# The drain of a two-stage expert pipeline, reordered on four engines

## Chip, core and metric

One NeuronCore of a Trainium2 chip runs the whole kernel. The metric is the device time of one execution in microseconds; the median of several runs is given. The profile comes from one execution of its own.

## What is computed

For each of 128 samples of 64 rows and 256 columns, two layers run one after the other. Each sample has an index for each layer.

```
# layer 0: expert e = itok_B_0_7[b] of 8
h = gelu(x @ Wi[e] + bi[e])                 # 256 -> 1024
r = h @ Wo[e] + bo[e] + x                   # 1024 -> 256
x = layernorm(r, 1e-12) * gamma[e] + beta[e]
# layer 1: domain d = itok_B_0_15[b] of 16
a = gelu(x @ down_W.T + down_b)             # 256 -> 64
a = a @ expert_W[d].T + expert_b[d] + domain_emb[d]
x = layernorm(a @ up_W.T + up_b + x, 1e-5) * ln_gamma + ln_beta
```

## The kernel before

The samples are sorted by expert on the chip and laid into 68 tiles of two samples each (128 rows). A tile passes through a software pipeline: step `i` works on tiles `i` down to `i - 5` at once, on all engines, and each engine runs its own written order of operations; semaphores alone tie the engines together. Steps 0 to 67 start a tile each; steps 68 to 72 only finish tiles, and are called the drain here. Step numbers of the drain are Python integers, as are those from 64 on (from 66 on in SyncE's queue); earlier steps run in loops.

For a tile `t` the stages and the step in which they run:

- Step t, TensorE: first product into `p_h` (L929 to L931). ScalarE: gelu (L589) and rounding to 16 bits (`h_hi`, L597), in two halves. VectorE: the rest `h_lo` (L775), the first half in step t, the second in step t + 1.
- Step t + 1, TensorE: second product into the one bank `p_o` (L1028, then 24 matmuls L937 to L939). It may start when the residual sum of the tile before has been read out of `p_o`.
- Step t + 2, VectorE: residual sum r (L785), its statistics (L788, L797); GpSimd: variance to the power -1/2 (L488); VectorE: z = normalized r (L816), into the one buffer `z1`; TensorE: two transposes of z into `p_t` (L970), written between the two halves of the second product of tile t + 1; GpSimd: fetches gamma and beta of the expert into `gb_tile` (L496); ScalarE: `yT` from the transposes (L629).
- Step t + 3, TensorE: down projection (L948); ScalarE: gelu (L613) and 16 bit part (L616); VectorE: low part `a1s` (L805); GpSimd: `yg` = z times gamma of the expert (L483).
- Step t + 4, TensorE: up projection (L958, then four L962) into `p_u`; VectorE: second residual sum into `yg` (L794), statistics (L800, L808); GpSimd: power (L492); VectorE: normalized y (L825).
- Step t + 5, GpSimd: times the last gamma (L475), plus the last beta (L477); SyncE: two transfers to `out` (L379).

In one step the order on GpSimd is: L475 and L477, L483, L488, L492, L496, and where they exist the copies for tile i (L502, L461). On VectorE it is: L785, L788, L794, L797, L800, L805, L808, L775 (second half), L816, the low part of x, L825, and the first half L775. TensorE's step begins with loading registers and addresses for the weights; up and down projections lie inside the first product, and in the drain, where no first product exists, they stand at the beginning of the step. Before writing z for tile i - 2, VectorE waits for the transposes of the tile before and for GpSimd's multiply (L483) of the tile before (`need(dve, yg_done, i - 2)`).

Of the kernel before, what the change touches and what calls it, by code (L numbers as in the profile page):

```python
# [4 lines left out]
B, S, D = 128, 64, 256  # L5
# [3 lines left out]
KD, KI = D // P, I // P  # L9
# [29 lines left out]
def build(nc, t):  # L39
# [4 lines left out]
    with ctx:  # L44
# [6 lines left out]
        def sem(name):  # L51
            return ctx.enter_context(nc.semaphore(name))
# [190 lines left out]
        z2_done = sem("z2_done")  # L243
        zg_done = sem("zg_done")
        y_done = sem("y_done")

        block = ctx.enter_context(nc.Block())

# [27 lines left out]
        def run(eng, step, unroll=4, ahead=0):  # L276

            lead, mid = LEAD - ahead, CHUNKS - FIRST_CHUNKS - ahead
            for i in range(lead):
                j = i + ahead  # L280
                step(i, i % 2, i % 4, (j % NCH, (j + FIRST_CHUNKS) // NCH, j % SLOTS_W))
            tail = mid + (TILES - 2 - mid) // 4 * 4
            for begin, end, weights, times in ((lead, mid, True, unroll), (mid, tail, False, 4)):
                with eng.Fori(0, (end - begin) // times) as n:
                    i = eng.snap(n * times + begin)
                    for q in range(times):
                        step(i + q, q % 2, (begin + q) % 4,
                             (q, n + (FIRST_CHUNKS + LEAD) // NCH, (LEAD + q) % SLOTS_W) if weights else False)
            for i in range(tail, STEPS):
                step(i, i % 2, i % 4, False)  # L290

        def loads(i, parity, each):

# [13 lines left out]
        def _(sp):  # L307
# [59 lines left out]
            def step(i, parity, four, weights):  # L367
                if weights:
                    if weights[0] == 0:
                        expert[0] = first_chunk(weights[1])  # L370
                    load_later(i + AHEAD, expert[0], weights[0], weights[2])
                if exists(i + 2) or exists(i - 5):
                    b = indices(sp, 6 * i + IDX_SP, 6, SLOTS - 1)
                if exists(i + 2):
                    load_turned(inside(b[2:4]), i + 2, parity)
                if exists(i - 5):
                    sp.wait_ge(y_done, i - 4)
                    for n in range(2):
# [11 lines left out]
        def _(pool):  # L390
# [73 lines left out]

            def step(i, parity, four, weights):
                e_third, e_before, _, _, e_next = indices(pool, i + (IDX_EXP - 3), 5, E0 - 1)
                if exists(i - 5):

                    last = y[:, 1 - parity, :]
                    pool.wait_ge(z2_done, i - 4)  # L470

                    pool.wait_ge(hlo_half, 2 * min(i, TILES) - 1 if isinstance(i, int) else 2 * i - 1)
                    if isinstance(i, int) and i == 5:
                        pool.wait_ge(ln_in, 2 * 16)
                    pool.tensor_tensor(last, last, lng[:, :], ALU.mult).then_inc(zg_done, 1)  # L475
                    pool.wait_ge(zg_done, i - 4)
                    pool.tensor_tensor(last, last, lnb[:, :], ALU.add).then_inc(y_done, 1)  # L477
                if exists(i - 3):

                    if isinstance(i, int) and i == 3:  # L480
                        pool.wait_ge(g_in, 16)
                    pool.wait_ge(z1_done, i - 2)
                    pool.tensor_tensor(yg[:, 1 - parity, :], z1[:, :], g_t[:, bass.ds(e_third * D, D)], ALU.mult)\  # L483
                        .then_inc(yg_done, 1)
                if exists(i - 2):

                    pool.wait_ge(mv1_done, i - 1)
                    pool.tensor_tensor(rs[:, 0:1], mv[:, 0, 1:2], neg_half[:, 0:1], ALU.pow).then_inc(rs1_done, 1)  # L488
                if exists(i - 4):

                    pool.wait_ge(mv2_done, i - 3)
                    pool.tensor_tensor(rs[:, 1:2], mv[:, 1, 1:2], neg_half[:, 0:1], ALU.pow).then_inc(rs2_done, 1)  # L492
                if exists(i - 2):

                    need(pool, yT_done, i - 2)
                    pool.tensor_copy(gb_tile[:, :], gb_c[:, bass.ds(e_before * 2 * KD, 2 * KD)]).then_inc(gb_done, 1)  # L496
                if exists(i):

                    if isinstance(i, int) and i == 0:
                        pool.wait_ge(sel_ready, 1)  # L500
                    need(pool, up_done, i - 3)
                    pool.tensor_copy(sel_tile[:, four, :].rearrange("p (n s) -> p n s", n=2),  # L502
                                     sel[:, bass.ds(2 * i, 2)].unsqueeze(2).to_broadcast([P, 2, S]))\
                        .then_inc(sel_done, 1)
                if exists(i + 1):
                    gather_bi(e_next, i + 1, 1 - parity)
                if isinstance(i, int) and i == 1:
                    pool.wait_ge(u_ready, 1)
# [129 lines left out]
        def _(dve):  # L638
# [139 lines left out]
            def step(i, parity, four, weights):  # L778
                if isinstance(i, int) and i == 0:
                    dve.wait_ge(bo_ready, 1)  # L780
                if exists(i - 2):

                    dve.wait_ge(s2_done, i - 1)
                    dve.wait_ge(xnat_in[parity], loads(i - 2, parity, 2))
                    v.scalar_tensor_tensor(r1[:, :], p_o[:, 0:D], 1.0 / (HS * WS), x_nat[:, parity, :],  # L785
                                           ALU.mult, ALU.add).then_inc(r1_done, 1)
                    dve.wait_ge(r1_done, i - 1)
                    v.bn_stats(st1[:, 0:6], r1[:, :]).then_inc(st1_done, 1)  # L788
                    dve.wait_ge(st1_done, i - 1)
                if exists(i - 4):  # L790

                    dve.wait_ge(up_done, i - 3)
                    dve.wait_ge(yg_done, i - 3)
                    v.scalar_tensor_tensor(yg[:, parity, :], p_u[:, 0:D], 1.0 / (AS * CS), yg[:, parity, :],  # L794
                                           ALU.mult, ALU.add).then_inc(r2_done, 1)
                if exists(i - 2):
                    v.bn_aggr(mv[:, 0, :], st1[:, :]).then_inc(mv1_done, 1)  # L797
                if exists(i - 4):
                    dve.wait_ge(r2_done, i - 3)
                    v.bn_stats(st2[:, 0:6], yg[:, parity, :]).then_inc(st2_done, 1)  # L800
                    dve.wait_ge(st2_done, i - 3)
                if exists(i - 3):

                    dve.wait_ge(a1_hi, i - 2)
                    v.scalar_tensor_tensor(own(S), a1[S:P, :].rearrange("p (n s) -> p n s", n=2), AS, own(S),  # L805
                                           ALU.mult, ALU.subtract).then_inc(a1_lo, 1)
                if exists(i - 4):
                    v.bn_aggr(mv[:, 1, :], st2[:, :]).then_inc(mv2_done, 1)  # L808
                if exists(i - 1):
                    split_h(i - 1, 1 - parity, 1)  # L810
                if exists(i - 2):

                    dve.wait_ge(rs1_done, i - 1)
                    need(dve, tr_done, i - 2)
                    need(dve, yg_done, i - 2)
                    v.tensor_scalar(z1[:, :], r1[:, :], mv[:, 0, 0:1], rs[:, 0:1], ALU.subtract, ALU.mult)\  # L816
                        .then_inc(z1_done, 1)
                if exists(i + 1):
                    low_x(i + 1, 1 - parity)
                if exists(i - 4):  # L820

                    dve.wait_ge(rs2_done, i - 3)
                    if not isinstance(i, int) or i >= 6:
                        dve.wait_ge(y_out[parity], loads(i - 6, parity, 2))
                    v.tensor_scalar(y[:, parity, :], yg[:, parity, :], mv[:, 1, 0:1], rs[:, 1:2],  # L825
                                    ALU.subtract, ALU.mult).then_inc(z2_done, 1)
                if weights:

                    dve.wait_ge(w_hi, i + 1)
# [9 lines left out]
        def _(pe):  # L839
# [101 lines left out]
            def step(i, parity, four, weights):  # L941
# [85 lines left out]
                        pe.wait_ge(bo_ready, 1)  # L1027
                    mm(p_o[:, 0:D], sel_tile[:, (four + 3) % 4, :], bo_parts[:, :], start=True, stop=False)  # L1028
                for j in range(KI):
                    if j == TR_AT and exists(i - 2):  # L1030
                        transpose()
                    if exists(i - 1):
                        if j == KI // 2:
# [1 line left out]
                        ins = second_product(1 - parity, there, j)  # L1035
                        if j == KI - 1:
                            ins.then_inc(s2_done, 1)

            pe.wait_ge(idx_ready, TILE_READY)
            run(pe, step)  # L1040
# [47 lines left out]
```

## Time and profile before

| | us |
|---|---|
| median of 3 runs (498.99 to 499.26) | 499.21 |
| the profiled execution's own time | 498.85 |
| its span, first to last instruction | 497.1 |
| TensorE busy with matmuls | 473.9 (95%) |
| VectorE busy | 355.6 (72%) |
| GpSimd busy | 358.6 (72%) |
| mean granted clock of TensorE | 0.983 |

The span is the stretch between the first and the last instruction of the profiled execution; its own time holds 1.75 us around it. The profile names each operation by its line in the kernel, with start, duration, and in brackets how long the engine had been idle before it and what released it. PE is TensorE's matmuls, PEld its weight loads, DVE VectorE, ACT ScalarE, POOL GpSimd, SPq SyncE's queue.

### The profile page before, as it was taken

Reading aid. Unit: us, or ns where it says so; the run is one execution under the profiler, and the core shown is the slowest. Engines: PE = TensorE matmul, PEld = TensorE weight load, DVE = VectorE, ACT = ScalarE, POOL = GpSimd, SP = SyncE. Lnnn points to the kernel's source line nnn. Section 1 sums busy time; section 2 is a strip of 40 time slices with the busy share of each in tenths; the row PEclk is TensorE's granted clock in tenths of the full one; section 3 lists DMA queues with packets and bytes.
Section 4 is the critical chain, followed back from the end, with each engine's and each line's share of the span. In section 5 each row is a group of like instructions: output and inputs, shape, how many; then the busy total and the mean of one; then the engine's idle time right before and its main releaser. Section 6 shows DMA issues by size and latency. Waiting matters only on the chain.

```text
span 497.1 us, 19258 instructions
## 1 busy us (share of the span) xinstructions
PE 473.9 (95%) x5778; PEld 438.7 (88%) x5779; DVE 355.6 (72%) x936; ACT 373.8 (75%) x1099; POOL 358.6 (72%) x587
## 2 busy tenths in 40 slices
PE   4699999999999999999999999999999999999972
PEld 2399999999999999999999999999999999999961
DVE  6678777777777777777777777777777767666662
ACT  2588887777787778788777778877878877677651
POOL 6044787788778877788778877887778876667765
PEclk9799999999999999999999999999999999999996
DMA  4734343333343333333333333333343222222111
GB/s 117 269 83 117 93 91 105 100 95 99 102 106 105 86 99 100 98 96 103 103 88 95 99 100 99 102 86 102 97 100 79 63 55 66 64 58 55 39 44 32
DMA packets 70257, 45.84 MB, mean 92 GB/s; under 512 B 43969, under 2 KB 61778, under 8 KB 70098
## 3 DMA queue, kind: packets, MB, share of 16 engines
q1 hardware_dynamic: 69200, 45.25, 34.6%
q8 instruction: 15, 0.25, 0.2%
q10 hardware_dynamic: 1026, 0.21, 0.2%
q14 instruction: 16, 0.13, 0.1%
HBM read 36.51 MB, written 8.91 MB: 91 GB/s over the span
## 4 chain that ended last, share of the span: by engine, by line
PE 93%; DVE 3%; POOL 1%; issue 1%; DMA 0%; ACT 0%; POOLq 0%; DVEq 0%
PE p_h L929 13%; PE p_h L931 12%; PE p_h L930 12%; PE p_o L939 12%; PE p_o L938 12%; PE p_o L937 12%; PE p_d L948 7%; PE p_u L962 6%; PE p_t L970 3%; PE p_u L958 2%; PE p_o L1028 1%; PE p_h L872 1%; DVE W L737 1%; POOL y L475 0%; PE p_t L872 0%
## 5 line engine op out<-in xcount | busy, mean ns | idle before, releaser
L929 PE MATMUL p_h<-x_hi,W 128*128 128x128 f16 x1088 | 193.8, 220 | 0.0
L930 PE MATMUL p_h<-x_lo,W 128*128 128x128 f16 x1088 | 193.6, 220 | 0.0
L931 PE MATMUL p_h<-x_hi,W 128*128 128x128 f16 x1088 | 193.6, 220 | 0.0
L589 ACT ACTIVATE h<-p_h,bi_tile 128x128 f32<-128x128 f32 x544 | 152.6, 362 | 0.6 <-PE p_h L931 0.6
L938 PE MATMUL p_o<-W,h_hi 128*128 x544 | 148.3, 273 | 0.0
L939 PE MATMUL p_o<-W,h_lo 128*128 x544 | 148.3, 273 | 0.0
L937 PE MATMUL p_o<-W,h_hi 128*128 x544 | 148.3, 273 | 0.0
L492 POOL TENSOR_TENSOR rs<-mv,neg_half 128x1 f32<-128x1 f32 x68 | 59.7, 878 | 74.2 <-DVE mv L808 74.2
L929 PEld LDWEIGHTS p_h<-x_hi,W 128*128 x1088 | 107.0, 98 | 5.2 <-issue 3.8
L930 PEld LDWEIGHTS p_h<-x_lo,W 128*128 x1088 | 106.9, 98 | 2.1
L931 PEld LDWEIGHTS p_h<-x_hi,W 128*128 x1088 | 106.9, 98 | 0.0
L613 ACT ACTIVATE a<-p_d,downb 128x128 f32<-128x128 f32 x68 | 25.0, 367 | 90.0 <-PE p_d L948 90.0
L775 DVE SCALAR_TENSOR_TENSOR h_lo<-h,h_hi 128x512 f16<-128x512 f32 x136 | 91.1, 670 | 1.4 <-ACT h_hi L597 1.4
L597 ACT ACTIVATE h_hi<-h 128x512 f16<-128x512 f32 x136 | 86.1, 633 | 2.2
L502 POOL COPY sel_tile<-sel 128x128 f16 (+1 forms) x68 | 81.0, 1191 | 2.0 <-issue 2.0
L805 DVE SCALAR_TENSOR_TENSOR a1s<-a,a1s 64x128 f16<-64x128 f32 x68 | 19.7, 289 | 66.5 <-ACT a1s L616 66.4
L475 POOL TENSOR_TENSOR y<-y,lng 128x256 f32<-128x256 f32 x68 | 49.3, 726 | 20.5 <-DVE h_lo L775 18.7
L785 DVE SCALAR_TENSOR_TENSOR r<-p_o,x_nat 128x256 f32<-128x256 f32 x68 | 28.8, 424 | 44.2 <-PE p_o L939 44.1
L939 PEld LDWEIGHTS p_o<-W,h_lo 128*128 128x128 f16 x544 | 53.2, 98 | 6.2
L938 PEld LDWEIGHTS p_o<-W,h_hi 128*128 128x128 f16 x544 | 53.2, 98 | 6.2
L629 ACT ACTIVATE yT<-p_t,gb_tile 128x128 f32<-128x128 f32 x136 | 55.3, 461 | 3.7 <-PE p_t L970 2.1
L937 PEld LDWEIGHTS p_o<-W,h_hi 128*128 128x128 f16 x544 | 53.2, 98 | 4.7
(155 smaller groups left out, 814.3 us busy)
## 6 DMA issues: line engine op xcount, KB each, us to landing
stage<-in_w SPq DMA_DIRECT2D x56, 256.0 KB, 2.7
x_nat<-in_x SPq DMA_DIRECT2D x136, 64.0 KB, 2.1
out<-y SPq DMA_DIRECT2D x136, 64.0 KB, 2.0
x_T<-in_xT SPq DMA_DIRECT2D x134, 64.0 KB, 2.2
W<-in_w SPq DMA_DIRECT2D x8, 256.0 KB, 4.6
g_t<-in_gamma SPq DMA_DIRECT2D x1, 1024.0 KB, 7.8
W<-in_expert_W SPq DMA_DIRECT2D x2, 128.0 KB, 3.0
upT<-in_up_W SPq DMA_DIRECT2D x2, 64.0 KB, 2.7
```

What stands on the lines that cost most here:

```text
L492: pool.tensor_tensor(rs[:, 1:2], mv[:, 1, 1:2], neg_half[:, 0:1], ALU.pow).then_inc(rs2_done, 1)
L502: pool.tensor_copy(sel_tile[:, four, :].rearrange("p (n s) -> p n s", n=2), sel[:, bass.ds(2 * i, 2)].unsqueeze(2).to_broadcast([P, 2, S]))\
L589: ins = nc.scalar.activation(h[:, c, :], p_h[parity][:, c, :], ACT.Gelu, bias=bi_tile[:, parity, c:c + 1], scale=1.0 / (XS * WS))
L597: nc.scalar.activation(h_hi[:, parity, cols_h, :], h[:, cols_h, :], ACT.Copy, scale=HS)\
L629: ins = nc.scalar.activation(yT[:, k, :], p_t[:, k * P:k * P + P], ACT.Identity, bias=gb_tile[:, KD + k:KD + k + 1], scale=gb_tile[:, k:k ...
L775: v.scalar_tensor_tensor(h_lo[:, parity, cols_h, :], h[:, cols_h, :], HS, h_hi[:, parity, cols_h, :], ALU.mult, ALU.subtract).then_inc(hlo ...
L929: mm(p_h[parity][:, c, :], hi, x_hi[:, parity, k, :], start=(k == 0), stop=False)
L930: mm(p_h[parity][:, c, :], hi, x_lo[:, parity, k, :], start=False, stop=False)
L931: ins = mm(p_h[parity][:, c, :], lo, x_hi[:, parity, k, :], start=False, stop=(k == KD - 1))
L937: mm(p_o[:, 0:D], h_hi[:, parity, j, :], hi, start=False, stop=False)
L938: mm(p_o[:, 0:D], h_hi[:, parity, j, :], lo, start=False, stop=False)
L939: return mm(p_o[:, 0:D], h_lo[:, parity, j, :], hi, start=False, stop=(j == KI - 1))
```

## The change

All of it concerns the drain (steps 68 and later) and the outputs of the last four tiles (64 to 67). TensorE: the second product of tile 67 runs without the transposes in its middle; the transposes stand behind it. GpSimd in the drain: first the copy to `gb_tile`, then both powers, then the multiply by the expert's gamma, then the output's gamma and beta, and these last two not at all for the last four tiles. VectorE in the drain: a new order, beginning with the second half of `h_lo`, and for the last four tiles the output in two fused operations, (yg - mean) * ln_gamma and then times the power plus ln_beta. SyncE waits for a semaphore of its own for these four.

```
 GpSimd, step(i):
+                if drain(i):                    # i an int, i >= 68
+                    gather_gb()
+                    powers()
+                    scale_z()
+                    scale_out()                 # only if the tile i - 5 is none of the last four
+                else:
+                    scale_out()
+                    scale_z()
+                    powers()
+                    gather_gb()
...
 VectorE, step(i):
+                def late_gamma():
+                    dve.wait_ge(mv2_done, i - 3)
+                    dve.wait_ge(y_out[parity], loads(i - 6, parity, 2))
+                    v.scalar_tensor_tensor(y[:, parity, :], yg[:, parity, :], mv[:, 1, 0:1], lng[:, :],
+                                           ALU.subtract, ALU.mult).then_inc(yl_done, 1)
+                def late_out():
+                    dve.wait_ge(rs2_done, i - 3)
+                    dve.wait_ge(yl_done, i - 3 - (TILES - 4))
+                    v.scalar_tensor_tensor(y[:, parity, :], y[:, parity, :], rs[:, 1:2], lnb[:, :],
+                                           ALU.mult, ALU.add).then_inc(y_late, 1)
+                if drain(i):
+                    if exists(i - 1):
+                        split_h(i - 1, 1 - parity, 1)
+                    if exists(i - 2):
+                        residual_1()
+                        aggr_1()
+                    if exists(i - 4):
+                        residual_2()
+                        stats_2()
+                        aggr_2()
+                    if exists(i - 2):
+                        normal_1()
+                    if exists(i - 4):
+                        late_gamma()
+                    if exists(i - 3):
+                        low_a()
+                    if exists(i - 4):
+                        late_out()
+                    return
...
 TensorE, step(i), in and behind the second product:
-                    if j == TR_AT and exists(i - 2):
+                    if j == TR_AT and exists(i - 2) and not drain(i):
                         transpose()
...
+                if drain(i) and exists(i - 2):
+                    transpose()
...
 SyncE, step(i), in front of the output of tile i - 5:
-                    sp.wait_ge(y_done, i - 4)
+                    if late(i - 5):
+                        sp.wait_ge(y_late, i - TILES)
+                    else:
+                        sp.wait_ge(y_done, i - 4)
```

The functions `residual_1`, `aggr_1`, `residual_2`, `stats_2`, `normal_1` and `low_a` hold the operations that stood there before (L785 and L788, L797, L794, L800, L816, L805), `aggr_2` L808. Outside of the drain their order is the old one.

## Rows read from the trace of the kernel before

**Rows 1.** Page: the chain that ended last, shares of the span by engine.
```profile
PE 93%; DVE 3%; POOL 1%; issue 1%; DMA 0%; ACT 0%; POOLq 0%; DVEq 0%
```

**Rows 2.** Chain that ended last: start us, us, what.
```profile
491.27 0.56 POOL rs L492
...
493.11 0.76 POOLq L44
```

**Rows 3.** Timeline of VectorE, 476 us on: start us, us, operation, count.
```profile
476.92 0.42 DVE L785 SCALAR_TENSOR_TENSOR r<-p_o,x_nat 128x256 f32<-128x256 f32 x1 [1.21 <-PE p_o L939]
...
479.19 0.65 DVE L775 SCALAR_TENSOR_TENSOR h_lo<-h,h_hi 128x512 f16<-128x512 f32 x1
479.75 0.41 DVE L816 TENSOR_SCALAR z<-r,mv,rs 128x256 f32<-128x256 f32 x1
...
482.00 0.42 DVE L785 SCALAR_TENSOR_TENSOR r<-p_o,x_nat 128x256 f32<-128x256 f32 x1 [1.31 <-PE p_o L939]
...
484.27 0.37 DVE L816 TENSOR_SCALAR z<-r,mv,rs 128x256 f32<-128x256 f32 x1
...
488.12 0.29 DVE L805 SCALAR_TENSOR_TENSOR a1s<-a,a1s 64x128 f16<-64x128 f32 x1 [0.37 <-ACT a1s L616]
...
489.63 0.42 DVE L794 SCALAR_TENSOR_TENSOR yg<-p_u,yg 128x256 f32<-128x256 f32 x1
...
490.54 0.20 DVE L808 BATCH_NORM_AGGREGATE mv<-st 128x2 f32<-128x9 f32 x1
```

**Rows 4.** Timeline of TensorE (PE) and its weight loads (PEld), 477 us on.
```profile
477.60 0.10 PEld L1028 LDWEIGHTS p_o<-bo_parts,sel_tile 128*128 128x128 f16 x1
...
480.22 0.44 PE L970 MATMUL p_t<-ident,z 128*128 128x128 f32 x2 [0.93 <-DVE z L816]
...
481.69 0.27 PE L939 MATMUL p_o<-W,h_lo 128*128 x1
...
484.70 0.44 PE L970 MATMUL p_t<-ident,z 128*128 128x128 f32 x2 [1.75 <-DVE z L816]
486.09 0.10 PEld L958 LDWEIGHTS p_u<-parts,sel_tile 128*128 128x128 f16 x1 [1.19 <-issue]
...
486.23 0.60 PE L962 MATMUL p_u<-ctab,a1s 128*128 x4
...
488.47 1.03 PE L962 MATMUL p_u<-ctab,a1s 128*128 x4 [0.48 <-DVE a1s L805]
```

**Rows 5.** Timeline of GpSimd (POOL), 477 us on.
```profile
477.34 0.73 POOL L483 TENSOR_TENSOR yg<-z,g_t 128x256 f32<-128x256 f32 x1
...
479.35 0.89 POOL L492 TENSOR_TENSOR rs<-mv,neg_half 128x1 f32<-128x1 f32 x1 [0.36 <-DVE mv L808]
...
493.15 0.72 POOL L477 TENSOR_TENSOR y<-y,lnb 128x256 f32<-128x256 f32 x1
```

**Rows 6.** Timeline of ScalarE (ACT), 476 us on.
```profile
476.31 0.63 ACT L597 ACTIVATE h_hi<-h 128x512 f16<-128x512 f32 x1
```

**Rows 7.** Timeline of GpSimd and VectorE early in the run, 39.8 to 46 us.
```profile
39.87 0.68 DVE L737 SCALAR_TENSOR_TENSOR W<-stage,W 128x512 f16<-128x512 f32 x1
39.92 1.22 POOL L483 TENSOR_TENSOR yg<-z,g_t 128x256 f32<-128x256 f32 x1 [0.26 <-DVE z L816]
...
45.30 0.73 POOL L483 TENSOR_TENSOR yg<-z,g_t 128x256 f32<-128x256 f32 x1 [1.47 <-DVE z L816]
45.37 1.22 DVE L737 SCALAR_TENSOR_TENSOR W<-stage,W 128x512 f16<-128x512 f32 x1
```

**Rows 8.** Timeline of GpSimd and VectorE, 307 to 308 us.
```profile
307.14 0.50 DVE L825 TENSOR_SCALAR y<-yg,mv,rs 128x256 f32<-128x256 f32 x1
307.21 0.29 POOL L502 COPY sel_tile<-sel 128x128 f16 x1
```

**Rows 9.** Busy time by window: PE, PEld, DVE, ACT, POOL, granted clock, DMA.
```profile
487.00:487.25 0.25, 0.25 (x3) 0.08 (x1) 0.25 (x1) 0.00 (x0) 0.25 (x2) 1.00 0.00 0
487.25:487.50 0.25, 0.02 (x1) 0.00 (x0) 0.22 (x2) 0.19 (x1) 0.25 (x1) 0.69 0.00 0
```

More of the change, by code:

```diff
@@ L245, in build @@
         y_done = sem("y_done")
+        yl_done = sem("yl_done")
+        y_late = sem("y_late")
         block = ctx.enter_context(nc.Block())
@@ L290, in run, with drain, late @@
                 step(i, i % 2, i % 4, False)
+        def drain(i):
+            return isinstance(i, int) and i >= TILES
+        def late(j):
+            return isinstance(j, int) and TILES - 4 <= j < TILES
         def loads(i, parity, each):
@@ L466, in step @@
                 e_third, e_before, _, _, e_next = indices(pool, i + (IDX_EXP - 3), 5, E0 - 1)
[L467 to L496, printed above, removed]
+                def scale_out():
+                    if exists(i - 5) and not late(i - 5):
+                        last = y[:, 1 - parity, :]
+                        pool.wait_ge(z2_done, i - 4)
+                        pool.wait_ge(hlo_half, 2 * min(i, TILES) - 1 if isinstance(i, int) else 2 * i - 1)
+                        if isinstance(i, int) and i == 5:
+                            pool.wait_ge(ln_in, 2 * 16)
+                        pool.tensor_tensor(last, last, lng[:, :], ALU.mult).then_inc(zg_done, 1)
+                        pool.wait_ge(zg_done, i - 4)
+                        pool.tensor_tensor(last, last, lnb[:, :], ALU.add).then_inc(y_done, 1)
@@ new lines, in scale_z, with powers @@
+                def scale_z():
+                    if exists(i - 3):
+                        if isinstance(i, int) and i == 3:
+                            pool.wait_ge(g_in, 16)
+                        pool.wait_ge(z1_done, i - 2)
+                        pool.tensor_tensor(yg[:, 1 - parity, :], z1[:, :], g_t[:, bass.ds(e_third * D, D)], ALU.mult)\
+                            .then_inc(yg_done, 1)
+                def powers():
+                    if exists(i - 2):
+                        pool.wait_ge(mv1_done, i - 1)
+                        pool.tensor_tensor(rs[:, 0:1], mv[:, 0, 1:2], neg_half[:, 0:1], ALU.pow).then_inc(rs1_done, 1)
+                    if exists(i - 4):
+                        pool.wait_ge(mv2_done, i - 3)
+                        pool.tensor_tensor(rs[:, 1:2], mv[:, 1, 1:2], neg_half[:, 0:1], ALU.pow).then_inc(rs2_done, 1)
@@ new lines, in gather_gb @@
+                def gather_gb():
+                    if exists(i - 2):
+                        need(pool, yT_done, i - 2)
+                        pool.tensor_copy(gb_tile[:, :], gb_c[:, bass.ds(e_before * 2 * KD, 2 * KD)]).then_inc(gb_done, 1)
+                if drain(i):
[8 more added lines that the diff above has]
+                    gather_gb()
@@ L780, in step, with residual_1 @@
                     dve.wait_ge(bo_ready, 1)
-                if exists(i - 2):
+                def residual_1():
                     dve.wait_ge(s2_done, i - 1)
@@ L789, in step, with residual_2 @@
                     dve.wait_ge(st1_done, i - 1)
-                if exists(i - 4):
+                def residual_2():
                     dve.wait_ge(up_done, i - 3)
@@ L795, in step, with aggr_1, stats_2 @@
                                            ALU.mult, ALU.add).then_inc(r2_done, 1)
-                if exists(i - 2):
+                def aggr_1():
                     v.bn_aggr(mv[:, 0, :], st1[:, :]).then_inc(mv1_done, 1)
-                if exists(i - 4):
+                def stats_2():
                     dve.wait_ge(r2_done, i - 3)
@@ L801, in step, with low_a @@
                     dve.wait_ge(st2_done, i - 3)
-                if exists(i - 3):
+                def low_a():
                     dve.wait_ge(a1_hi, i - 2)
@@ L806, in step, with aggr_2, normal_1 @@
                                            ALU.mult, ALU.subtract).then_inc(a1_lo, 1)
-                if exists(i - 4):
+                def aggr_2():
                     v.bn_aggr(mv[:, 1, :], st2[:, :]).then_inc(mv2_done, 1)
-                if exists(i - 1):
-                    split_h(i - 1, 1 - parity, 1)
-                if exists(i - 2):
+                def normal_1():
                     dve.wait_ge(rs1_done, i - 1)
@@ L817, in step, with normal_2 @@
                         .then_inc(z1_done, 1)
-                if exists(i + 1):
-                    low_x(i + 1, 1 - parity)
-                if exists(i - 4):
+                def normal_2():
                     dve.wait_ge(rs2_done, i - 3)
@@ L826, in step @@
                                     ALU.subtract, ALU.mult).then_inc(z2_done, 1)
+                def late_gamma():
[11 more added lines that the diff above has]
+                        split_h(i - 1, 1 - parity, 1)
+                    if exists(i - 2):
+                        residual_1()
[4 more added lines that the diff above has]
+                        aggr_2()
+                    if exists(i - 2):
+                        normal_1()
+                    if exists(i - 4):
+                        late_gamma()
+                    if exists(i - 3):
+                        low_a()
+                    if exists(i - 4):
+                        late_out()
+                    return
+                if exists(i - 2):
+                    residual_1()
+                if exists(i - 4):
+                    residual_2()
+                if exists(i - 2):
+                    aggr_1()
+                if exists(i - 4):
+                    stats_2()
+                if exists(i - 3):
+                    low_a()
+                if exists(i - 4):
+                    aggr_2()
+                if exists(i - 1):
+                    split_h(i - 1, 1 - parity, 1)
+                if exists(i - 2):
+                    normal_1()
+                if exists(i + 1):
+                    low_x(i + 1, 1 - parity)
+                if exists(i - 4):
+                    normal_2()
                 if weights:
```

## The prediction

> **What bounds the kernel now.** I read the page first. The chain that ended last [rows 1] is TensorE's own work for 93% of the span, and nothing that the diff touches runs otherwise there, since every new branch asks whether the step number is a Python integer of 68 or more (or the output tile is one of the last four). So the whole effect lies in steps 68 to 72, the drain. I therefore read the end of the chain of waits [rows 2]: in the last 10 us it goes through GpSimd (power, gamma multiply, beta add) with VectorE between them, and a closing stretch in which the output lands. Then I read the timeline of each engine from 476 us on [rows 3 to 6]. Tiles are counted 0 to 67; "z(66)" is L816 for tile 66, "up(66)" L958 and L962, "down" L948, "r2" L794.
>
> The drain before: the second product of tile 67 begins at 477.60, breaks after its first half, waits for z(66), transposes at 480.22 and goes on to 481.96 [rows 4]. Then r(67) at 482.00, z(67) at 484.27 [rows 3], transposes at 484.70, up(66) at 486.09, the low part of the adapter input at 488.12 to 488.41, up(67) behind it, mean and variance of tile 67 done at 490.74, and from there GpSimd's power (started only at 491.27, because the beta add of tile 66 is in its way), normalization, gamma, beta, to 493.87 [rows 2, 3, 5]. The span ends 3.23 us after that: the output's issue and landing.
>
> **What the change gives.** *Last tile.* From 490.74 to 493.87 are 3.13 us. After: the power takes 0.55 [rows 2], and one fused operation of VectorE 0.42 (size of r, [rows 3]). For hand-overs I put 0.08 from VectorE to GpSimd, 0.04 back and to TensorE, 0.10 from ScalarE (all are sizes that the timeline has everywhere). Sum 1.09 us, with the mean-and-gamma operation beside the power. That one reads two SBUF tensors, and here a collision costs: with such an operation running, GpSimd's power takes 0.89 instead of 0.55 and ends 0.40 after it (479.84 to 480.24, [rows 3, 5]). The mean-and-gamma operation starts 0.05 before the power, so power ends at 0.03 + 0.42 + 0.40 = 0.85 and the output at 0.85 + 0.04 + 0.42 = 1.31. Gain 3.13 - 1.31 = **1.82 us** (2.04 without collision). Eight operations leave GpSimd, four more stand on VectorE.
> *Last product.* It loses its break of 1.2 us, but VectorE now does the low half of h (L775) before r(66). The high half ends at 476.94 [rows 6]; L775 starts 0.10 later, r(66) 0.56 behind it, at 477.60 instead of 476.92, ends 478.02, and the product, which waits for r(66) to leave p_o, starts at 478.07 instead of 477.60. Unbroken, 25 matmuls one every 0.109 us (from four in 0.60, the last 0.27 long, [rows 4]) take 3.00 us with the first load, and it ends at 481.07 instead of 481.96. So 0.89 us can be gained, if VectorE comes to r(67) then.
>
> **What it costs: z waits for GpSimd.** z1 is one buffer. z(66) may be written only when GpSimd has multiplied z(65) by gamma (L483). Before, that is done at 478.07, ahead of the powers (first row of [rows 5]). Now it stands behind both powers, and the second of them waits for the statistics of tile 64, on VectorE.
> Step 68: r(66) 477.60, then its statistics, r2(64) and its statistics in 0.46 + 0.46 + 0.12 + 0.46 + 0.46 + 0.20 us (spacing of the same operations: from r at 476.92 to the last behind them, L775 at 479.19, are 2.27 us with L805's 0.32 between, [rows 3]): 479.76. Power 479.84 to 480.39, multiply of z(65) to 481.08. z(66) could start at 481.12 instead of 479.75.
> There a second collision: GpSimd goes straight on to the gamma multiply of y(63), from 481.04, before VectorE starts. What that does is shown early in the run [rows 7]: L483 starts at 45.30, L737 at 45.37, and L737 takes 1.22 us where it takes 0.68 elsewhere, ending 0.56 us after GpSimd's end; the other way round, L483 started behind L737 takes 1.22 instead of 0.73. Is z, with one SBUF tensor, of that kind? L825, the same sort of operation, took 0.50 instead of 0.41 beside a GpSimd copy and ended 0.14 after it [rows 8]. I take that: z(66) ends 0.14 after 481.77, at **481.91 instead of 480.16 (+1.75)**; without the collision 481.53.
> The Trainium skill (SBUF — State Buffer, section "Who interferes with whom") says that a VectorE instruction with two SBUF inputs, or in a two-port mode, and a GpSimd instruction that reads SBUF exclude each other for the whole instruction, the first to issue winning. By it the sum has its three collisions, and without it 0.82 us less; rows 7 agree with it.
>
> *From z(66) to z(67).* The transposes now wait at the end of TensorE's step, so what the queue does at the start of the next step can't begin before z(66) is there. The price is in [rows 4]: transposes at 484.70, up(66) loaded at 486.09, put down to issue: 1.39 us (before, the second half of the product hid this once, up to its last matmul at 481.69). So transposes 481.95, up(65) 483.34, and r2(65) can follow 0.78 later (486.09 to the end of L962 at 486.83, and 0.04): 484.12. VectorE: mean-and-gamma, low part, output of tile 64 take 0.9 us of starts and meet GpSimd's beta add of y(63), one blocking of 0.6; r(67) starts at about 483.3 (before: 482.00, so the product's 0.89 us is lost), and r2(65) 1.04 behind it, 484.35. Statistics 1.11 later (489.63 to 490.74, [rows 3]) 485.46, power to 486.09, multiply of z(66) 486.05 to 486.78, z(67) **486.82 instead of 484.27 (+2.55)**.
> *From z(67) to the low part of tile 67.* z(67) ends 487.23, transposes 487.27, up(66) 488.66. In the profile of before this stretch, 486.09 to 488.41, takes 2.32 us, and TensorE does it just before its granted clock falls from 1.00 (2.4 GHz) to 0.50 (1.2 GHz), at 487.3 [rows 9]. The fall came 5.3 us behind the end of the product at 481.96, and TensorE had mostly waited in between. In the new order the product ends at 481.07 and up(66) comes 7.6 us later, so I expect the clock to be down when up(66) and down(67) run. At 1.2 GHz four L962 matmuls take 1.03 instead of 0.60 [rows 4], so 0.107 more for each in the stream; five of up(66) ahead of down(67), three more in down, and a tail of 0.10: 0.54 + 0.32 + 0.10 = 0.95. The down matmuls at the lower clock are not in the trace; bounds are 0 and 1.3 (double of all nine and their tail). Low part done: 488.66 + 2.32 + 0.95 = **491.93 instead of 488.41 (+3.52)**.
> *End.* Up(67) is at 1.2 GHz in both, and the way to the statistics the same 2.33 us: 494.26. Output 1.31 later: **495.57 instead of 493.87 (+1.70)**. Against the profiled execution's span of 497.1 (its own time 498.85, 0.36 below the median of the runs) that is 498.8; on the median of 499.21, **500.9 us**.
> Costed at nothing: SyncE (the output of tile 63 goes some 5 us later, but its buffer is needed again only for tile 65, after 487, and issue and landing are about 3.2 us), the gb_tile copy ahead of the powers (it waits for yT of tile 65, and GpSimd idles there), and two more semaphores.
>
> **Rivals.**
> 1. *No collisions*: GpSimd and VectorE pass each other. z(66) 0.38 earlier, 0.22 less in step 68, 0.22 less at the last power: +0.88, 500.1, within 0.2%. Rows 7 speak against it; for it, that z is not a two-tensor operation. 0.17.
> 2. *The clock holds* until up(67) is through: 0.95 and 0.43 less (an up with its four L962 in 1.03 instead of 0.60): +0.32, 499.5. Against it: the fall came 5.3 us behind the product, and up(67) would lie 10.9 us behind it. A partial case is that it falls late enough for up(66) alone. 0.10.
> 3. *The clock falls before up(65)*: 0.5 more there: 501.4. 0.08.
> 4. *Faster*: z(66) does not wait for the multiply of z(65) beyond 481.1, the end of the product. Then the transposes follow without a gap, the issue time is hidden behind the product, r(67) starts at 481.11, all of the later work comes 0.89 earlier and the tail is 1.82 shorter: -2.7, 496.5. For it speaks only the intent of the order; against it, that the second power stands in front and can't start before 479.8. 0.05.
> Mine: 0.60, with 500.3 to 501.5 as its own range.
>
> **Numbers.** 0.2% is 1.0 us, about what this kernel's measurement can tell from no change. Slower: mine and rival 3, 0.68. Same: rivals 1 and 2, 0.27. Faster: rival 4, 0.05. The range reaches from rival 2 to above rival 3 with another blocked operation of 0.6: 499.4 to 501.9.
>
> **What would show it.** (a) The last product has no gap, starts 0.4 to 0.5 later and ends near 481.1. (b) L816's equal for tile 66 is released by GpSimd's multiply, near 481.1, and is longer than 0.41. (c) 1.4 us of issue behind each of the last two pairs of transposes. (d) z(67) near 486.8. (e) TensorE's clock at 0.50 by up(66). (f) From the last statistics to the last output 1.1 to 1.3 us. I am wrong if z(66) starts before 480, if up(65) follows its transposes at once, or if up(66) and down(67) run at full clock.

## The result and the profile after

The changed kernel takes 500.7 us in the median of 17 runs (499.88 to 501.04), the kernel before 499.26 (17 runs beside them, 498.93 to 500.72). The ratio is 1.0023, 95% interval 1.0016 to 1.0031: slower by 0.8 to 1.5 us. Forecast were 500.9. The profiled execution took 500.62 us, its span is 498.9 against 497.1.

In the new listing r is L820, z L858, the low part L846, the last statistics L851, the output pair L873 and L880; on GpSimd the multiply of z is L501, the powers are L509 and L513, gamma and beta of the output L490 and L492; on TensorE the transposes are L1065, up L1053 and L1057, down L1043, the second product L1123 and L1032 to L1034.

VectorE's timeline, drain (start us, duration us, operation, and what ended its idle time), to be held against [rows 3]:

```profile
481.19 0.69 DVE L858 TENSOR_SCALAR z<-r,mv,rs 128x256 f32<-128x256 f32 x1 [1.46 <-POOL yg L501]
481.80 1.01 DVE L873 SCALAR_TENSOR_TENSOR y<-yg,mv,lng 128x256 f32<-128x256 f32 x1
...
483.56 0.42 DVE L820 SCALAR_TENSOR_TENSOR r<-p_o,x_nat 128x256 f32<-128x256 f32 x1
...
487.13 0.41 DVE L858 TENSOR_SCALAR z<-r,mv,rs 128x256 f32<-128x256 f32 x1 [1.45 <-POOL yg L501]
487.45 0.48 DVE L873 SCALAR_TENSOR_TENSOR y<-yg,mv,lng 128x256 f32<-128x256 f32 x1
...
491.97 0.29 DVE L846 SCALAR_TENSOR_TENSOR a1s<-a,a1s 64x128 f16<-64x128 f32 x1
...
494.30 0.20 DVE L851 BATCH_NORM_AGGREGATE mv<-st 128x2 f32<-128x9 f32 x1
494.53 0.51 DVE L873 SCALAR_TENSOR_TENSOR y<-yg,mv,lng 128x256 f32<-128x256 f32 x1
495.16 0.48 DVE L880 SCALAR_TENSOR_TENSOR y<-y,rs,lnb 128x256 f32<-128x256 f32 x1
```

Both z of the drain are released by GpSimd's multiply after 1.46 and 1.45 us of idle time; before, neither waited for it. GpSimd's timeline, against [rows 5]:

```profile
479.81 0.55 POOL L513 TENSOR_TENSOR rs<-mv,neg_half 128x1 f32<-128x1 f32 x1 [0.45 <-DVE mv L851]
480.32 0.73 POOL L501 TENSOR_TENSOR yg<-z,g_t 128x256 f32<-128x256 f32 x1
481.00 0.72 POOL L490 TENSOR_TENSOR y<-y,lng 128x256 f32<-128x256 f32 x1
481.81 0.72 POOL L492 TENSOR_TENSOR y<-y,lnb 128x256 f32<-128x256 f32 x1
...
494.58 0.55 POOL L513 TENSOR_TENSOR rs<-mv,neg_half 128x1 f32<-128x1 f32 x1 [1.74 <-DVE mv L851]
```

TensorE's timeline (PE matmuls, PEld weight loads), against [rows 4]:

```profile
478.26 0.10 PEld L1123 LDWEIGHTS p_o<-bo_parts,sel_tile 128*128 128x128 f16 x1 [0.55 <-issue]
...
480.90 0.27 PE L1034 MATMUL p_o<-W,h_lo 128*128 x1
481.93 0.44 PE L1065 MATMUL p_t<-ident,z 128*128 128x128 f32 x2 [0.76 <-DVE z L858]
...
483.32 0.10 PEld L1053 LDWEIGHTS p_u<-parts,sel_tile 128*128 128x128 f16 x1 [1.19 <-issue]
...
487.59 0.69 PE L1065 MATMUL p_t<-ident,z 128*128 128x128 f32 x2 [3.09 <-DVE z L858]
...
488.98 0.10 PEld L1053 LDWEIGHTS p_u<-parts,sel_tile 128*128 128x128 f16 x1 [1.10 <-issue]
...
489.17 1.06 PE L1057 MATMUL p_u<-ctab,a1s 128*128 x4
...
490.03 1.06 PE L1043 MATMUL p_d<-yT,downT 128*128 128x128 f32 x4
```

The product has no break and ends at 481.17, and nothing takes it up: r(67) starts at 483.56. Behind each pair of transposes stand 1.39 us until the next up projection loads. Up(66) and down(67) take 1.06 us each at the end, since the granted clock (third number from the right) has fallen by then, as the windows say, against [rows 9]:

```profile
486.00:486.50 0.50, 0.00 (x0) 0.00 (x0) 0.00 (x0) 0.00 (x0) 0.50 (x2) 1.00 0.00 0
486.50:487.00 0.50, 0.00 (x0) 0.00 (x0) 0.00 (x0) 0.00 (x0) 0.49 (x1) 0.75 0.55 131
487.00:487.50 0.50, 0.00 (x0) 0.00 (x0) 0.37 (x2) 0.00 (x0) 0.00 (x0) 0.50 0.46 111
```

The milestones of the two executions, us:

| | before | forecast | after |
|---|---|---|---|
| end of the last product | 481.96 | 481.07 | 481.17 |
| end of z(66) | 480.16 | 481.91 | 481.88 |
| start of z(67) | 484.27 | 486.82 | 487.13 |
| end of the low part of tile 67 | 488.41 | 491.93 | 492.26 |
| end of its statistics | 490.74 | 494.26 | 494.50 |
| end of the last output operation | 493.87 | 495.57 | 495.64 |

### The profile page after: what moved, and what is told of

Same layout as the page of the kernel before. It is cut to its first block, busy times and chain, and to the rows that moved or that the text cites. A ratio compares the mean times of both kernels' runs of the same rounds, so it can differ in the third digit from the quotient of the medians.

```text
span 498.9 us, 19251 instructions
## 1 busy us (share of the span) xinstructions
PE 474.8 (95%) x5778; PEld 438.8 (88%) x5779; DVE 359.7 (72%) x940; ACT 374.3 (75%) x1099; POOL 352.6 (71%) x579
## 4 chain that ended last, share of the span: by engine, by line
PE 89%; DVE 3%; issue 3%; POOL 2%; ACT 2%; DMA 0%; POOLq 0%; DVEq 0%; ACTq 0%
PE p_h L1024 12%; PE p_h L1025 12%; PE p_h L1026 12%; PE p_o L1034 11%; PE p_o L1032 11%; PE p_o L1033 11%; PE p_d L1043 7%; PE p_u L1057 6%; PE p_t L1065 3%; PE p_u L1053 2%; PE p_o L1123 1%; ACT h L624 1%; PE p_h L967 1%; DVE W L772 0%; POOL yg L501 0%
## 5 line engine op out<-in xcount | busy, mean ns | idle before, releaser
L1032 PE MATMUL p_o<-W,h_hi 128*128 x544 | 148.3, 273 | 0.0
L1034 PE MATMUL p_o<-W,h_lo 128*128 x544 | 148.3, 273 | 0.0
L513 POOL TENSOR_TENSOR rs<-mv,neg_half 128x1 f32<-128x1 f32 x68 | 59.3, 871 | 79.6 <-DVE mv L851 79.6
L846 DVE SCALAR_TENSOR_TENSOR a1s<-a,a1s 64x128 f16<-64x128 f32 x68 | 19.7, 289 | 66.2 <-ACT a1s L651 66.1
L490 POOL TENSOR_TENSOR y<-y,lng 128x256 f32<-128x256 f32 x64 | 46.5, 727 | 17.8 <-DVE h_lo L810 17.8
L820 DVE SCALAR_TENSOR_TENSOR r<-p_o,x_nat 128x256 f32<-128x256 f32 x68 | 28.8, 424 | 41.7 <-PE p_o L1034 41.6
L1034 PEld LDWEIGHTS p_o<-W,h_lo 128*128 128x128 f16 x544 | 53.2, 98 | 6.2
L1032 PEld LDWEIGHTS p_o<-W,h_hi 128*128 128x128 f16 x544 | 53.2, 98 | 4.6
```

The lines of the kernel that those rows point to most:

```text
L1032: mm(p_o[:, 0:D], h_hi[:, parity, j, :], hi, start=False, stop=False)
L1034: return mm(p_o[:, 0:D], h_lo[:, parity, j, :], hi, start=False, stop=(j == KI - 1))
```

## The experiments

The start of the drain (the start of ScalarE's last `h_hi` operation) lies between 475.27 and 476.68 in the profiled executions, though up to there all kernels run the same operations. So beside the medians I give the *stretch*, from that start to the end of the last output operation. It is 17.56 us before and 19.30 after. The stretch is one execution's, the median is that of 4 to 17 executions. The ten kernels of the experiments ran in three batches with the kernel before beside them, whose medians were 499.10, 499.13 and 499.04; differences to the kernel before are taken within a batch. before_second_look and before_third_look are one more profiled execution each of the kernel before.

| kernel | median us | ratio to before, 95% | stretch us |
|---|---|---|---|
| after | 500.70 | 1.0023 (1.0016 to 1.0031) | 19.30 |
| multiply_before_powers | 497.47 | 0.9971 (0.9960 to 0.9982) | 16.32 |
| transposes_in_the_middle | 500.78 | 1.0038 (1.0025 to 1.0052) | 20.16 |
| output_pair_alone | 497.42 | 0.9965 (0.9953 to 0.9977) | 16.59 |
| old_output_first | 499.83 | 1.0017 (1.0008 to 1.0026) | 18.84 |
| gpsimd_order_alone | 506.04 | 1.0137 (1.0121 to 1.0152) | 24.46 |
| fillers_in_tensore | 499.45 | 1.0010 (1.0001 to 1.0019) | 18.48 |
| multiply_first_old_output_first | 497.34 | 0.9962 (0.9948 to 0.9976) | 16.34 |
| pair_alone_and_fillers | 496.92 | 0.9958 (0.9944 to 0.9971) | 15.72 |
| gpsimd_old_order | 496.47 | 0.9947 (0.9933 to 0.9960) | 15.24 |
| gpsimd_old_order_and_fillers | 495.99 | 0.9934 (0.9920 to 0.9947) | 14.90 |

**multiply_before_powers.** The changed kernel with one line moved, and a wait for the operation that last reads the multiply's buffer:

```
 drain, GpSimd:
                     gather_gb()
+                    scale_z()
                     powers()
-                    scale_z()
                     scale_out()
...
 scale_z, behind its wait for z1_done:
+                        if drain(i):
+                            pool.wait_ge(z2_done if i == TILES else yl_done, TILES - 4 if i == TILES else i - TILES)
```

> The changed kernel, with GpSimd's multiply of z by the expert's gamma ahead of both powers in the drain (and the waits that keep its buffer free). My theory: the place behind the second power is what costs. Then z(66) ends at 480.2 instead of 481.88, the transposes stand right behind the last product, no issue gap ahead of up(65), up(66) loads near 485.3 and not 488.98, last output near 491.1 to 491.4: median 496.2 to 496.8, some 2.7 us below the kernel before. Rival (the loss lies in the new orders of VectorE and TensorE, not in this wait): 500 to 501.

Measured: 497.47, some 3.2 us below the changed kernel and 1.6 below the kernel before, so the place of the multiply is the loss. It is 0.7 above the forecast range. The transposes do stand right behind the product, but GpSimd's operations now meet others of VectorE: the multiply of z(65), from 476.47, meets the low half of h, and the old output of tile 63 meets the low part and the output. VectorE's timeline:

```profile
476.62 1.12 DVE L812 SCALAR_TENSOR_TENSOR h_lo<-h,h_hi 128x512 f16<-128x512 f32 x1 [1.27 <-ACT h_hi L634]
...
480.53 0.82 DVE L848 SCALAR_TENSOR_TENSOR a1s<-a,a1s 64x128 f16<-64x128 f32 x1
481.38 0.90 DVE L882 SCALAR_TENSOR_TENSOR y<-y,rs,lnb 128x256 f32<-128x256 f32 x1
482.21 0.41 DVE L822 SCALAR_TENSOR_TENSOR r<-p_o,x_nat 128x256 f32<-128x256 f32 x1
```

The low half of h takes 1.12 instead of 0.69, the low part 0.82 instead of 0.29 and the output operation 0.90 instead of 0.48, and r(67) starts at 482.21, with the product through at about 481.

**gpsimd_order_alone.** The kernel before, and of the change only GpSimd's order in the drain (outputs of all tiles still on GpSimd):

```
                 if drain(i):
                     gather_gb()
                     powers()
                     scale_z()
                     scale_out()
...
 def late(j):
-            return isinstance(j, int) and TILES - 4 <= j < TILES
+            return False
```

> The kernel before with only GpSimd's new order in the drain (copy, both powers, multiply of z, then output gamma and beta, for all tiles); VectorE, TensorE and the output as before. My theory: the multiply behind the second power holds z back here too, and the old outputs collide with z: z(66) ends near 481.7, z(67) near 487.8, last output 3.5 to 4.2 us later than before: median 502.7 to 503.4, the whole loss of the change without its gain. Rival (the loss comes from the three new orders together): 499 to 500.

Measured: 506.04, 7 us above the kernel before. The direction was right, the size missed by 3 us. z(66) ended at 482.13 and the statistics of tile 67 at 495.96: from the start of the drain that is 4.85 us more than before, with up(66) and down(67) at 1.06, and from there to the last output come another 2.05. These last are what I had not counted at all (VectorE's timeline):

```profile
499.13 0.41 DVE L866 TENSOR_SCALAR y<-yg,mv,rs 128x256 f32<-128x256 f32 x1 [3.17 <-DMA out<-y]
```

With the outputs last on GpSimd, the output of tile 65 was sent at 496.3 and tile 67, which shares its buffer, waited 3.17 us for the transfer. In the changed kernel tile 67's output operation (L873) starts 0.03 behind its statistics, without such a wait. So of the 7 us not more than 4.85 can be laid to the place of the multiply.

**output_pair_alone.** The orders of the kernel before on all engines, with the output pair in the place of the normalization, and the wait that multiply_before_powers has too:

```
-                if exists(i - 4):
+                if exists(i - 4) and drain(i):
+                    late_gamma()
+                    late_out()
+                elif exists(i - 4):
                     normal_2()
```

> Of the change only the output of the last four tiles in two VectorE operations; the orders of the three engines as in the kernel before. My theory: nothing ahead of the statistics of tile 67 (490.74) moves, and from there to the last output it is 1.14 us instead of 3.13: -2.0 us, median 497.2. Rival (the pair collides with GpSimd's power, 1.31 or more): 497.4 to 498. Rival (the output pair delays VectorE's earlier work in the drain, at L785 or L794, by more than 0.5 each): 498.5 to 499.

Measured: 497.42, 0.2 us off, and by the median alone just inside the first rival's range; the trace decides against that rival, since the statistics of tile 67 end at 491.35 and the last output at 492.49, 1.14 us as in my theory. So this part of the change is worth about its estimate by itself: 1.7 in the medians. In this profile up(66) ran at the low clock, where the profile of the kernel before shows 0.60:

```profile
485.89 1.06 PE L1043 MATMUL p_u<-ctab,a1s 128*128 x4
```

**transposes_in_the_middle.** `and not drain(i)` and the `transpose()` behind the product are taken out of the changed kernel.

> The changed kernel with the transposes of z(66) back in the middle of the last product. My theory: z(66) is late (481.88) whatever TensorE does, the product then ends near 483.7 instead of 481.17, but r(67) starts at 483.56 anyway in the changed kernel because VectorE is held up, and the issue gap ahead of up(65) is hidden: within 0.3 us of the changed kernel, 500.4 to 501.0. Rival (the unbroken product is worth its 0.9 to 1.2 us): 501.6 to 501.9.

Measured: 500.78, within 0.1 us in the median, as my theory had it, but the ratio is 0.0015 higher and the stretch 0.86 longer, which is not. The trace tells why. TensorE (matmuls), and two windows:

```profile
481.19 0.44 PE L1065 MATMUL p_t<-ident,z 128*128 128x128 f32 x2 [2.06 <-DVE z L858]
...
482.50 0.42 PE L1034 MATMUL p_o<-W,h_lo 128*128 x1
...
483.57 1.06 PE L1057 MATMUL p_u<-ctab,a1s 128*128 x4
```

```profile
481.50:482.00 0.50, 0.50 (x7) 0.45 (x5) 0.50 (x1) 0.34 (x1) 0.29 (x1) 1.00 0.00 0
482.00:482.50 0.50, 0.50 (x5) 0.36 (x3) 0.44 (x3) 0.47 (x2) 0.00 (x0) 0.65 0.00 0
```

TensorE waited 2.06 us in the middle of the product, the clock fell at 482.1, in the product's second half, and those matmuls came 0.21 apart and not 0.11; r(67) waited for them. Up(65) did follow the product at once (483.36), so the issue gap was hidden as expected. Product without a break: worth something, through the clock; how much between 0 and 0.9 us is not settled by median and ratio together. In this execution the clock was back at 1.00 from about 485.6 to 489.0, while TensorE did little but two transposes, and fell a second time ahead of up(66) (489.29, 1.06 us):

```profile
485.00:485.50 0.50, 0.48 (x3) 0.19 (x1) 0.47 (x2) 0.00 (x0) 0.35 (x1) 0.50 0.00 0
...
488.00:488.50 0.50, 0.15 (x2) 0.00 (x0) 0.44 (x3) 0.31 (x1) 0.00 (x0) 1.00 0.00 0
...
489.00:489.50 0.50, 0.37 (x2) 0.28 (x3) 0.00 (x0) 0.00 (x0) 0.00 (x0) 0.50 0.00 0
```

**old_output_first.** The changed kernel with `scale_out()` moved to the head of GpSimd's drain order.

> The changed kernel with the gamma and beta of y(63) at the head of GpSimd's step 68 (where GpSimd idles) and not behind the multiply of z(65). Takes away the collisions with z(66) and the first output operation (0.69 and 1.01 us long in the changed kernel instead of 0.41 and 0.42). My theory: z(66) 0.38 earlier, r2(65) and all behind it 0.85 earlier: 499.8. Rival (what is gained is taken up again by the wait of z(67) for GpSimd): 500.5 to 500.8.

Measured: 499.83 in the median; by the stretch 0.46 earlier and not 0.85. z(66) and the output operation are down to 0.41 and 0.48, but a collision came in elsewhere:

```profile
475.94 0.96 DVE L810 SCALAR_TENSOR_TENSOR h_lo<-h,h_hi 128x512 f16<-128x512 f32 x1 [1.27 <-ACT h_hi L632]
```

0.96 instead of 0.69, beside GpSimd's beta add and copy, at the head of everything: z(66) ended 5.53 us behind the start of `h_hi`, against 5.54 in the changed kernel. Only the collision of the output operation, 0.5 us, was gained.

**fillers_in_tensore.** The changed kernel with matmuls that nobody reads where TensorE waits in the drain:

```
+                def filler(n):
+                    for _ in range(n):
+                        mm(ph_flat[0][:, 0:D], h_hi[:, 0, 0, :], w_flat[NCH // 2][:, 0:D], start=True, stop=True)
...
                         down()
+                        if drain(i) and i > 68:
+                            filler(24 if i == 69 else 10)
...
                 if drain(i) and exists(i - 2):
                     transpose()
+                    if isinstance(i, int) and i == 69:
+                        filler(8)
```

> The changed kernel with 42 matmuls more on TensorE whose result nobody reads, in the places where it waits in the drain (24 behind the down projection of step 69, 8 behind the transposes of step 69, 10 behind the down projection of step 70). My theory: the granted clock stays at 1.00, up(66), down(67) and up(67) take 0.60, 0.61, 0.60 instead of about 1.05 each, and the last output comes 1.4 us earlier: 499.2 to 499.5. Rival (the clock is not on the path, the wait for GpSimd covers it): 500.5 to 500.9. Rival (the fillers get in the way): above 501.

Measured: 499.45, stretch 0.82 shorter. The clock held; busy time, clock and DMA of a window, and up(66):

```profile
488.00:490.00 2.00, 1.85 (x18) 1.48 (x17) 0.94 (x3) 0.63 (x3) 0.00 (x0) 1.00 0.12 30
```

```profile
488.79 0.60 PE L1057 MATMUL p_u<-ctab,a1s 128*128 x4
```

The clock is on the path. In the trace 0.82 us and not 1.4 come back, since VectorE is there too:

```profile
490.57 0.51 DVE L873 SCALAR_TENSOR_TENSOR y<-yg,mv,lng 128x256 f32<-128x256 f32 x1
491.11 0.29 DVE L846 SCALAR_TENSOR_TENSOR a1s<-a,a1s 64x128 f16<-64x128 f32 x1
491.43 0.83 DVE L880 SCALAR_TENSOR_TENSOR y<-y,rs,lnb 128x256 f32<-128x256 f32 x1
492.19 0.41 DVE L830 SCALAR_TENSOR_TENSOR yg<-p_u,yg 128x256 f32<-128x256 f32 x1
```

The low part of tile 67 (L846) follows VectorE's mean-and-gamma operation of tile 66 without idle time, and so it does already in the changed kernel (491.97, behind 491.43 to 491.94), where ScalarE was through at 491.84. That way hangs on up(66) alone and is 0.48 shorter; of up(67) come back 0.34 and not 0.43, since r2(67) now follows VectorE's output operation (L880).

**pair_alone_and_fillers.** output_pair_alone with 14, 8 and 8 such matmuls.

> As output_pair_alone (the order of the kernel before on all engines, only the output in two operations), with 30 such unread matmuls on TensorE (14, 8 and 8). In the profile of output_pair_alone up(66) and down(67) ran at 0.50, in that of the kernel before at 1.00. My theory: with the clock held, the low part of tile 67 is 0.95 earlier and up(67) 0.43 shorter: 496.0 to 496.5, and less spread between executions. Rival (clock off the path): 497.3 to 497.6.

Measured: 496.92, 0.5 us less in the median, 0.87 in the stretch, both less than the forecast of 0.9 to 1.4. In the trace the low part of tile 67 comes 0.86 earlier, but of up(67), 0.61 instead of 1.04, nothing comes back: in both kernels r2(67) follows VectorE's output operation of tile 66 without idle time. That the median gives less still may be because the clock is not down in every execution of this order, as the last two profiles show for the kernel before; for this pair it is not shown.

**multiply_first_old_output_first.** multiply_before_powers with `scale_out()` at the head.

> As multiply_before_powers, and the gamma and beta of y(63) at the head of GpSimd's step 68. In multiply_before_powers the low part of tile 65 and the last output operation of tile 64 took 0.82 and 0.90 us beside that gamma and beta, and r(67) came at 482.21, though the product was through near 481.1. My theory: r(67) follows the product, z(67) and all behind it come 0.9 to 1.1 earlier: 496.3 to 496.7. Rival (something else holds r(67)): 497.2 to 497.7.

Measured: 497.34, a miss by 0.6 at least, and in the rival's range, though r(67) did start with the product's end (480.76). The stretch is that of multiply_before_powers: z(67) now waited for a power that stood behind the copy and the multiply,

```profile
483.44 0.41 DVE L860 TENSOR_SCALAR z<-r,mv,rs 128x256 f32<-128x256 f32 x1 [0.51 <-POOL rs L511]
```

and up(66) and down(67) both took 1.06 (in multiply_before_powers up(66) still had 0.62).

**gpsimd_old_order and gpsimd_old_order_and_fillers.** The changed kernel with GpSimd's order of the kernel before (scale_out, scale_z, powers, gather_gb) and the wait above; the second also with 6, 8 and 8 unread matmuls.

> The changed kernel with GpSimd's order in the drain as in the kernel before (outputs, multiply of z, powers, copy to gb_tile), and the waits that keep the multiply's buffer free: VectorE's new order, the unbroken product and the output pair stay. In multiply_first_old_output_first z(67) waited until 483.44 for a power that stood behind the copy and the multiply, and VectorE was free at 482.94. My theory: z(67) and all behind it 0.4 to 0.5 earlier than there, 496.8 to 497.0; the clock is down for up(66) and down(67), so nothing more. Rival (the new order of VectorE loses as much as it gains against output_pair_alone): 497.3 to 497.6.

> As gpsimd_old_order, with 22 unread matmuls on TensorE (6, 8 and 8) where it waits in the drain. My theory: up(66), down(67) and up(67) at a granted clock of 1.00, 1.2 to 1.4 us less than gpsimd_old_order: 495.4 to 495.8, the fastest of all. Rival (22 are too few, the clock falls all the same): 496.8 to 497.0.

Measured: 496.47, 0.3 below the forecast range, and 495.99, 0.2 above it: the unread matmuls gave 0.48 and not 1.2 to 1.4. Up(66) of gpsimd_old_order ran at the high clock in its profile (0.60), so the fillers had only up(67) left to gain there. The second is the fastest version found: 3.0 us below the kernel before, 4.7 below the changed one. Against output_pair_alone, gpsimd_old_order has VectorE's new order and the unbroken product, and is 0.95 us faster in the median (ratios 0.9947 and 0.9965, whose intervals overlap); with the clock held in both, gpsimd_old_order_and_fillers is 0.93 faster than pair_alone_and_fillers, and its stretch is 0.82 shorter. So these two parts of the change gain together, once GpSimd doesn't hold z; their shares were not measured apart.

**before_second_look, before_third_look.** The kernel before, unchanged.

> The kernel before, unchanged, one more profile. In its first profile TensorE's clock fell at 487.3, just behind up(66) and down(67); with the same orders in output_pair_alone it fell before up(66), which then took 1.06 us. My theory: the place of the fall is not tied to the program, so in another execution up(66) can run at 0.50, with the last output 0.9 to 1.0 us later behind the same start of the drain; if it falls as in the first profile, the stretch from the start of r(66) to the last output is 16.95 us again. Rival: the place of the fall follows from the program alone; then it is at 487.3, and the stretch 16.95, in every profile of it.

> As before_second_look: one more profile of the kernel before. By my theory one of the two has the fall at another distance from r(66) than 10.4 us, by up to 3 us; by the rival both have 10.4 and a stretch of 16.95 us from r(66) to the last output.

Measured: 499.29 and 498.94. Up(66) and the window of the fall in the second profile:

```profile
485.79 1.06 PE L962 MATMUL p_u<-ctab,a1s 128*128 x4
```

```profile
485.50:486.00 0.50, 0.36 (x2) 0.28 (x3) 0.00 (x0) 0.11 (x1) 0.42 (x2) 0.69 0.00 0
```

and up(66) of the third:

```profile
486.31 0.60 PE L962 MATMUL p_u<-ctab,a1s 128*128 x4
```

In the second the clock fell some 9.3 us behind the start of r(66) instead of 10.4, ahead of up(66), and the stretch was 18.48 us; in the third it fell behind down(67) and the stretch was 17.57, as in the first (17.56). So 0.92 us of the drain of the kernel before hang on where the fall comes in the execution, and its first profile showed the good case. The second execution as a whole was only 0.44 us longer than the first (499.29 against 498.85), since its drain began 0.49 earlier.

## Why the prediction held

- *Multiply behind the powers*: as forecast. z(66) ended at 481.88 (forecast 481.91), released by the multiply; multiply_before_powers takes 3.2 us away, gpsimd_order_alone brings 7, of which 4.85 ahead of the last statistics.
- *Collision at z(66)*: as forecast. z lasted 0.69 and ended 0.16 after GpSimd's gamma multiply. The output operation of tile 64 behind it lasted 1.01 instead of 0.48, ending 0.28 after the beta add. The blocking, 0.53, was if anything below my 0.6. What I had too small is the starts of the three operations ahead of r(67): 0.9 us, where the same three take 0.51 + 0.32 + 0.40 = 1.23 unblocked. So r(67) came at 483.56 instead of 483.3, and with it z(67) 0.31 later than forecast. This is a mis-sized term, and it carried to the low part (492.26 against 491.93).
- *Issue gap*: 1.39 twice, as forecast. Only the second is on the path: up(65) ended at 484.06, and r2(65), held by VectorE, started at 484.59.
- *Lost clock*: from the load of up(66) to the end of the low part 3.28 us against 2.32, +0.96 (forecast 0.95; its terms 0.54, 0.32 and 0.10 add up to 0.96). The path was a tie: by TensorE and ScalarE the low part could have started at about 491.94, by VectorE it started at 491.97, and the forecast knew only the first of these. Down at 1.2 GHz, which was not to be seen before, takes 1.06 instead of 0.61.
- *Last tile*: 494.50 to 495.64 are 1.14 us, not 1.31. The third collision did not take place: power lasted 0.55 although the output operation had started 0.05 earlier, and that one took 0.51 instead of 0.48. The Trainium skill (SBUF — State Buffer, section "Who interferes with whom") has the first to issue hold the shared port for its whole instruction; by the recorded starts the power should then have been held up, and was not. The rows decide: a recorded lead of 0.05 us did not hold the power up, where 0.16 of L775 over L492 [rows 3, 5] did; whether the lead makes the difference or the other VectorE operation is not shown. Gain of the tail 1.99 instead of 1.82.
- *Sum*: +3.85 at the low part, 0.09 taken back before the statistics end (3.76), -1.99: +1.77 in the profiled executions, forecast 1.70. The sizes that were off (+0.33, -0.09 and -0.17) nearly cancelled, so that the sum came within 0.07 is in part luck.
- *Median*: the forecast laid the profiled difference on the median. Measured are 1.44 in the medians and 0.8 to 1.5 by the ratio. The three profiles of the kernel before offer a reason: the first had the late fall of the clock, which saves 0.92 us of the drain that the second didn't have. That this is what makes up the difference is argued, not shown; the third had the late fall as well.
- *Rivals*: no collisions (1) is refuted for two of the three (z took 0.69 and the output operation 1.01); the third, at the last power, indeed did not come. That the clock holds (2) and that it falls before up(65) (3) did not occur in the profile of the changed kernel; transposes_in_the_middle, where it falls even inside the product, shows a price of 0.86 in the stretch for the latter (forecast 0.5). The faster rival (4), -2.7, is what the change without its GpSimd order gives: -2.6 (gpsimd_old_order). That it hangs on the place of the multiply was right.

## What to carry to other kernels

When an engine's order is rewritten, look at the single buffers: an operation that frees one must not be put behind work that waits for a third engine, however early that work is wanted. Operations taken off the end of the chain (the output pair) gained about their sum, while a collision removed between VectorE and GpSimd turned up at another pair: even in the fastest version the low half of h takes 0.96 and the multiply of z 1.17. In a thin drain TensorE's clock is a term of the sum, and a few unread matmuls in its waits can buy it back, as far as no other engine is level with it.

## What was not expected of the hardware

The fall of TensorE's granted clock from 1.00 to 0.50 comes at different places of the same program: 10.4, 9.3 and 10.7 us behind the start of r(66) in three executions, costing 0.92 us of stretch when it comes ahead of up(66). In transposes_in_the_middle it fell at 482.1, was back at 1.00 by 486 and fell again near 489. With 42 unread matmuls it stayed at 1.00 in the profiled drain. And with starts 0.05 us apart, a VectorE operation with two SBUF inputs and a GpSimd power ran side by side (0.51 and 0.55 us).
